# Semaphore-only ends for the blocks of a two-layer attention and expert kernel, and its semaphores cleared in three places

## The reference

```python
x = x + xattn0(layernorm(x), ctx, ctx, mask)              # softmax(QK/4, -inf where mask) V, 512 queries, 1024 keys
x = x + ffn0(layernorm(x))                                # 8 experts, top 2, capacity 32 per group, gelu(x w0) * (x w1) w2
x = x + xattn1(layernorm(x), ctx, ctx, attn_mask, pad)    # the same, with an additive mask
x = x + ffn1(layernorm(x))                                # 8 experts, top 2 without capacity, silu(x g) * (x u) d
```

## Time and profile before

| | us |
|---|---|
| median of three runs | 1161.09 |
| lowest and highest run | 1156.19, 1162.87 |
| the profiled execution's own time | 1161.39 |
| its span (first to last instruction) | 1159.7 |
| TensorE busy | 1102.2 (95%) |
| VectorE busy | 546.3 (47%) |
| ScalarE busy | 492.9 (43%) |
| GpSimd busy | 486.8 (42%) |

### The profile page before, as it was taken

The page is one execution under the profiler, slowest core; times in us unless marked ns, Lnnn a source line. Parts: engine busy times, 40 slices in busy tenths (PEclk is TensorE's granted clock), DMA queues, the critical chain, the costliest instruction groups (busy, mean ns, idle before and its releaser), DMA issues. The chain is left out here.

```text
span 1159.7 us, 18943 instructions
## 1 busy us (share of the span) xinstructions
PE 1102.2 (95%) x6905; PEld 715.2 (62%) x6905; DVE 546.3 (47%) x1534; ACT 492.9 (43%) x738; POOL 486.8 (42%) x510
## 2 busy tenths in 40 slices
PE   7899999999899999999899999999994999999996
PEld 4553333332578888888775333333344999999996
DVE  4568787773641111111247877777445112112111
ACT  4447676777451111111144688888854111111110
POOL 4357888875038684000005344444503233333332
PEclk9889999999999999999989999999998999999999
DMA  8634222002265955444079422200005999899960
GB/s 217 166 96 83 46 42 42 1 1 83 102 217 141 354 200 190 150 150 129 3 237 233 76 42 44 47 17 1 1 19 174 371 376 349 304 327 313 306 218 2
DMA packets 89607, 170.10 MB, mean 147 GB/s; under 512 B 11058, under 2 KB 61444, under 8 KB 87092
## 3 DMA queue, kind: packets, MB, share of 16 engines
q1 hardware_dynamic: 80916, 157.33, 43.3%
q0 software_dynamic: 6048, 8.28, 2.9%
q10 hardware_dynamic: 2560, 3.41, 1.0%
HBM read 150.19 MB, written 19.54 MB: 146 GB/s over the span
## 5 line engine op out<-in xcount | busy, mean ns | idle before, releaser
L1482 ACT ACTIVATE prob<-st_ps 128x1024 f32<-128x1024 f32 x186 | 189.6, 1022 | 62.6 <-PE st_ps L1343 40.3
L246 DVE CUSTOM_DVE_ANT_0 junk<-s_ps,bias_rows,mx 128x512 f32<-128x512 f32 x240 | 169.9, 748 | 45.1 <-PE s_ps L231 45.1
L231 PE MATMUL s_ps<-k_stack,q_stack 97*128 97x512 bf16 x476 | 177.6, 385 | 2.6 <-ACT q_stack L275 2.1
L246 DVE CUSTOM_DVE_ANT_0 junk<-s_ps,bias_rows 128x512 f32<-128x512 f32 x236 | 154.6, 688 | 50.8 <-PE s_ps L231 50.4
L1343 PE MATMUL st_ps<-q_stack,k_stack 100*128 100x512 bf16 x512 | 171.3, 383 | 2.1 <-ACTq L1452 1.6
L1929 PE MATMUL h_ps<-expert_in,w 128*128 (+1 forms) x704 | 153.4, 379 | 1.2 <-ACT k_stack L1962 0.7
L1281 POOL TENSOR_TENSOR prob<-prob,keep_cols 128x1024 int32<-128x1024 int32 x56 | 132.3, 2364 | 34.6 <-ACT prob L1482 34.6
L1929 PEld LDWEIGHTS h_ps<-expert_in,w 128*128 128x128 f32 (+1 forms) x704 | 131.4, 187 | 21.9 <-issue 1.9
L1369 PE MATMUL o_ps<-prob,v_unit 128*32 128x512 f32 x1024 | 139.6, 599 | 2.6 <-ACT prob L1482 1.0
L231 PEld LDWEIGHTS s_ps<-k_stack,q_stack 97*128 97x128 bf16 x476 | 45.2, 98 | 139.5 <-DVE mx L246 95.6
L2364 ACT ACTIVATE silu<-gu_ps 128x512 f32<-128x512 f32 x46 | 27.5, 597 | 227.6 <-PE gu_ps L2301 227.6
(11 more groups left out here) (360 smaller groups left out, 1465.2 us busy)
## 6 DMA issues: line engine op xcount, KB each, us to landing
wg<-in_gateT SPq DMA_DIRECT2D x23, 1024.0 KB, 6.2
wu<-in_upT SPq DMA_DIRECT2D x23, 1024.0 KB, 9.3
wd<-in_downT SPq DMA_DIRECT2D x23, 1024.0 KB, 12.5
w<-in_w SPq DMA_DIRECT2D x16, 1368.0 KB
w<-in_w SPq DMA_DIRECT2D x8, 1280.0 KB
k_stack<-k_scr SPq DMA_DIRECT2D x16, 384.0 KB, 5.1
k_stack<-k_scr SPq DMA_DIRECT2D x16, 256.0 KB, 5.6
k_scr<-k_parts SPq DMA_DIRECT2D x24, 128.0 KB, 2.6
```

What stands on the lines that cost most here:

```text
L231: pe.matmul(self.ps[:, self.bank("job", u, j)], stack(self.pr.Q[b], MROW, i % 2, h, slice(qt * P, (qt + 1) * P)), stack(self.pr.K[b], MROW ...
L246: self.pr.nc.vector.tensor_tensor_reduce(out=self.junk[:, self.bank("job", u, j)], in0=self.ps[:, self.bank("job", u, j)], in1=self.m.bias ...
L1482: nc.scalar.activation(prob[:, n % 2, 2 * hp:2 * hp + 2], st_ps[:, 2 * hp:2 * hp + 2], ACT.Exp).then_inc(exp_done, 1)
```

## The change

The clear, and the all-engine barrier behind it, are now in `free_sems`, which `main_program` calls three times: after the whole of layer 0's attention, after `moe_capacity`, and at the end of the program, where the semaphores of layer 1's attention and of `moe_top2` are cleared together. `free_sems` uses the same two calls as before.

```diff
     @contextmanager
     def stage(self):
 
-
-        outer, self.sems = self.sems, []
         with ExitStack() as inner:
             yield inner
-        if self.sems:
-            self.nc.clear_and_free_semaphores(self.sems)
-            self.nc.all_engine_barrier()
-        self.sems = outer
+
+    def free_sems(self, kept):
+        self.nc.clear_and_free_semaphores(self.sems[kept:])
+        self.nc.all_engine_barrier()
+        del self.sems[kept:]
...
-        with nc.Block() as block:
+        with nc.Block(no_gpsimd_drain=True) as block:
...
+            kept = len(pr.sems)
             attention_layer(pr, 0)
+            pr.free_sems(kept)
             moe_capacity(pr)
+            pr.free_sems(kept)
             attention_layer(pr, 1)
         moe_top2(pr)
+        pr.free_sems(kept)
```

## The result

The changed kernel takes 1153.57 us (median of 20 runs, 1150.38 to 1157.03), the kernel before 1160.37 (20 runs, 1156.19 to 1165.47). The ratio is 0.9945, 95% interval [0.9932, 0.9958]: 6.4 us faster. The forecast was 1161.9, 0.8 us above before and so no change that could be told from none, in a range from 1155.5 to 1164.5. The measured time lies under that range.

The account below looks back on a forecast made before the run. The kernel was taken as a chain of TensorE work (95% busy) broken by block ends. Terms -2.5 + 1.14 + 0 + 0.68 + 1.5 = +0.8 us on 1161.39 gave 1162.2, 0.3 lower as median: 1161.9, range 1155.5 to 1164.5.

Parts of the forecast that it names:

- The first of these inherits the work: The drain in free_sems takes over the block drain's work: +0.68 us behind moe_capacity, +1.5 at the end.
- the drain under 0.2 us behind `moe_capacity`: Sign in the profile after: a GpSimd drain this short there would prove the inheritance of the drain's work wrong.
- the tail under 8 us: Sign: last matmul to span end, 9.6 us before, 11.6 forecast; under 8 would disprove the drain's work per DMA.
- the step of the 69 DMAs: At the end, GpSimd's last drain walks through every DMA issued since the previous drain: 83 ns each, 5.7 us.
- -4.35: Lower bound in us at the program's end, if no drain work is left after SyncE's wait.
- rival 3: The drains of free_sems don't do the block drain's work; sum -5.7 us, 1155.4; chance 0.08.
- rival 1: Last drain ends at a set moment after the last DMA, whoever asks; sum -0.7 us, 1160.4; chance 0.15.
- rival 2: Long last drain is the price of asking with a DMA in flight; sum -4.35 us, 1156.7; chance 0.17.
- Four ends of scopes: Clear and second barrier go behind opening, both attend and layer 1's attention; -2.5 us, range -2.1 to -2.9.
- Longer clears: Merged clears and their ranged drains take longer at layer 0's end and the program's end: +1.14 us.
- The form of the barrier: Semaphores alone replace GpSimd's drain at the block ends; 0 us, at most +0.5 for six blocks.
- Rival 4: At moe_capacity's entry a longer gap drops TensorE's clock; +0.7 to +1.3 us more, 1162.6 to 1163.2; chance 0.15.

Follow-up runs that it names:

- experiment 3: Kernel before, with GpSimd waiting until the last additions have landed (and, in moe_capacity, for VectorE's last sums) before it drains; ratio 1.0014.
- experiment 6: Kernel before plus a plain GpSimd drain at tile 13; GpSimd waits until its DMAs have landed before that and the last drain; 1165.24 us, single run.
- experiment 4: Changed kernel with one more all-engine barrier in free_sems ahead of the clear, so a plain GpSimd drain precedes the ranged one; 1162.23 us, ratio 1.0014.
- experiment 7: Kernel before, with GpSimd clearing one spare semaphore at tile 13 (a ranged drain and range clear); ratio 0.9958.
- experiment 8, hidden clears: Changed kernel with three clears moved into the following block's GpSimd stream, without the barriers behind them; 1153.15 us, ratio 0.9942.
- no drain: Kernel before with no_gpsimd_drain in all blocks, keeping its seven clears and their barriers; ratio 0.9965.
- drain midway: Kernel before plus one plain GpSimd drain behind the additions of tile 13 in the second expert network; ratio 1.0001.
- after again: The changed kernel measured once more, unaltered, against the kernel before; 1152.72 us, ratio 0.9919.
- merged clears: Kernel before with its clears in three places as in the change, each block keeping its GpSimd drain; ratio 0.9973.

## Why the prediction was wrong

**The step that failed** is "The first of these inherits the work", +0.68 behind `moe_capacity` and +1.5 at the end. The 83 ns for each DMA that stood ahead of it were right (experiments 3 and 6). So of the prediction's two signs, the drain under 0.2 us behind `moe_capacity` (0.11) told the truth on the inheritance, and the tail under 8 us (5.8) did not prove the step of the 69 DMAs wrong: it came because nobody inherited them. I took all of GpSimd's drains for one operation, as I argued for the count from the block's drains and for the inheritance from "another, plain one (line 70)". But the drain of the clear stands ahead of line 70's and is of another kind. The profile of before had a sign of it, which I used only as a price: its duration grows with the range, as no plain drain's does. Experiments 4 and 7 show what it does instead. With 0 in place of 0.68 and -4.35 in place of 1.5 the sum is rival 3's -5.7; measured -6.4, interval -7.9 to -4.9. I gave that rival 0.08 on the ground that a plain drain follows, and had not asked what the one between them leaves for it.

**Rivals 1 and 2**, by which the drain waits for something, fell with experiment 3. The Trainium skill's rule that the data has landed once the completion semaphore has its full count ("DMA: Bandwidth & Descriptors", section "Two DMAs through the same engine are not ordered") was used in the prediction for -4.35 at the end. That number came, but not for this reason: in experiment 3 the semaphore has its full count before the drain, and a plain drain still takes 5.69 us. No run here tests the rule itself.

**Four ends of scopes, -2.5.** Right in place: no clear near 78, 293, 857 and 873 us is left. TensorE's waits for the barriers (us in total, times, longest us) at both `project` blocks, at the entry of `moe_top2` and at that of `moe_capacity`, before:

```profile
PE o_tok_ps L1583 <- PEq L70: 3.3, 2, 1.7
PE xt_ps L2267 <- PEq L70: 2.1, 1, 2.1
```

and after:

```profile
PE o_ps L1385 <- PEq L69: 4.1, 1, 4.1
PE h_ps L1867 <- PEq L69: 2.6, 1, 2.6
PE o_tok_ps L1582 <- PEq L1202: 2.1, 2, 1.0
PE xt_ps L2266 <- PEq L1563: 1.5, 1, 1.5
```

They fell by 0.6 us at each `project` and at `moe_top2`, where the forecast from rows was 0.4, 0.7 and 0.6. At the fourth place, behind `opening`, TensorE's idle time before its first matmul of `attend` fell from 1.59 to 0.88 us, where 0.8 was forecast.

**Longer clears, +1.14.** Right: 589 and 720 ns were forecast for ranges of 102 and 126, 591 and 717 measured. For the ranged drains 212 and 249 were forecast, 209 and 222 measured. TensorE's wait at the entry of `moe_capacity` grew from 1.9 us to 2.6, as above.

**The form of the barrier, 0.** Right within a tenth at the end: the last block's release comes at 1149.5, 0.3 us behind SyncE's branch. The texts ahead of the result count six blocks. There are seven in order of time, from five lines; a term of 0 stays 0 by that.

**Rival 4, the clock.** Its event came: TensorE's clock at the entry of `moe_capacity` fell at 305.2 us, 0.3 ahead of the restart, where before it fell 1.1 us behind it, at 310.9. These are the stages of after that answer to the earlier trace rows:

```profile
304.00:306.00 2.00, 0.50 (x1) 0.50 (x2) 0.49 (x6) 0.54 (x1) 0.00 (x0) 0.80 0.00 0
306.00:308.00 2.00, 2.00 (x3) 0.66 (x2) 1.41 (x13) 1.97 (x3) 0.00 (x0) 0.50 0.72 156
308.00:310.00 2.00, 2.00 (x5) 0.90 (x4) 1.47 (x8) 1.35 (x4) 0.00 (x0) 0.85 1.01 421
```

But it also rose earlier, so that the low stretch is no longer than before. By these rows it lasts 0.8 + 2.0 + 0.6 = 3.4 us, and by the earlier trace rows 1.1 + 2.0 + 0.3 = 3.4 before, which the prediction had read as 2.6. From release to release `moe_capacity` takes 267.8 us before and 268.3 after: +0.5 at most, not the 0.7 to 1.3 of that rival.

## What to carry to other kernels

Ask of each drain, clear and barrier what the one ahead of it leaves to do: an equal instruction further down inherits nothing if another has struck the work out in between. Where GpSimd issues many DMAs and its drain is what ends last, count the DMAs since the last drain and multiply by 83 ns. Where all of them have been waited for by semaphore anyway, as here, end the block without it, or let a ranged drain and its clear come first. No run here has a kernel that relies on the drain. When a trace gives the cause of a cost to 3%, that says nothing on who pays it after the change.

## What the runs showed of the hardware

- GpSimd's plain drain costs about 82 ns for each DMA that GpSimd has issued since the last drain: 717 ns for 8, 2002 for 24, 3730 for 45, 5690 for 69, all with nothing in flight. With DMAs in flight 45 took 9.7 us once, which is unexplained; the last drains with 24 and 69, behind a last DMA in flight, took no more than its descriptors and the count (3.99 and 7.5).
- A drain that carries a range of semaphores doesn't do this work, and it or the range clear behind it takes the work off the list. It takes 0.11 us for a range of 43 and 0.22 for 126. Right behind other work of GpSimd it took longer: 1.93 us behind the making of a DMA (experiment 7), and 1.10 for a range of 78 in the stream of `moe_top2` (experiment 8, hidden clears). A range clear takes 44 ns for one semaphore, 264 for 43, 591 for 102 and 717 for 126.
- Whether TensorE's clock falls at a short gap differs from profile to profile. With a wait of 1.9 to 2.0 us at the entry of `moe_capacity`, three profiles show it fall to 1.2 GHz (before, wait first, no drain) and three don't (drain midway, nothing in flight, ranged midway). With 2.5 to 2.9 us it fell in all four (after, after again, merged clears, plain first), with 1.5 us in the one that there is (hidden clears) it didn't. Behind `opening` it was low in parts of four profiles of eleven (before, wait first, plain first, nothing in flight), and its fall there precedes the block's end. `attend` took 214.4 and 214.5 us in the first two of these, and 211.7 or 211.8 in the other nine.
